# Cross-attention on one core: the K projection in seven 64x64 products in place of eight, from the second head pair on

## What is computed

```python
Q = (x @ W_Q).reshape(1024, 16, 64); K = (ctx @ W_K).reshape(6404, 16, 64); V = (ctx @ W_V).reshape(6404, 16, 64)
attn = softmax(Q K^T / 8, over the 6404 keys)              # per head
out = concat_heads(attn @ V) @ W_O + x
out = (out - mean(out)) / sqrt(var(out) + 1e-5)            # per row
```

## Time and profile before

| | |
|---|---|
| median of 3 runs | 1600.99 us (1600.53 to 1601.82) |
| the profiled execution's own time | 1601.11 us |
| its span in the profile | 1599.3 us |
| granted clock of TensorE, mean | 0.999 |
| TensorE busy | 1590.5 us (99%) |
| VectorE busy | 1314.6 us (82%) |
| ScalarE busy | 835.4 us (52%) |
| GpSimd busy | 64.2 us (4%) |

### The profile page before, as it was taken

The page is one execution under the profiler, slowest core; times in us unless marked ns, Lnnn a source line. Parts: engine busy times, 40 slices in busy tenths (PEclk is TensorE's granted clock), DMA queues, the critical chain, the costliest instruction groups (busy, mean ns, idle before and its releaser), DMA issues.

```text
span 1599.3 us, 39500 instructions
## 1 busy us (share of the span) xinstructions
PE 1590.5 (99%) x17484; PEld 1073.0 (67%) x17484; DVE 1314.6 (82%) x1229; ACT 835.4 (52%) x828; POOL 64.2 (4%) x41
## 2 busy tenths in 40 slices
PE   9999999999999999999999999999999999999998
PEld 4576677766777667766677666776677766777435
DVE  7788788887888788887798878988789887888877
ACT  4445554555545555456544565445654455544653
POOL 0001000010000001000010000000000000000100
PEclk9999999999999999999999999999999999999999
DMA  4000000000000000000000000000000000000000
GB/s 162 3 2 9 1 2 9 2 10 1 10 2 1 10 1 10 2 1 9 1 10 2 2 9 2 10 2 2 9 1 10 2 9 2 1 10 2 9 2 15
DMA packets 13006, 14.26 MB, mean 9 GB/s; under 512 B 4784, under 2 KB 8624, under 8 KB 12832
## 3 DMA queue, kind: packets, MB, share of 16 engines
q1 hardware_dynamic: 12544, 11.36, 2.3%
q10 hardware_dynamic: 288, 0.33, 0.1%
HBM read 10.60 MB, written 0.59 MB: 7 GB/s over the span
## 4 chain that ended last, share of the span: by engine, by line
PE 98%; DVE 1%; ACT 0%; issue 0%; DVEq 0%; ACTq 0%
PE o_ps L484 44%; PE s_ps L467 42%; PE w_ps L549 6%; PE w_ps L532 5%; PE s_ps L616 0%; DVE inv_sum L943 0%; DVE y L976 0%; DVE stats L963 0%; PE w_ps L564 0%; DVE y L959 0%; PE w_ps L607 0%; DVE inv_sum L809 0%; DVE sums L835 0%; DVE limits L985 0%; DVE k_all L809 0%
## 5 line engine op out<-in xcount | busy, mean ns | idle before, releaser
L728 ACT ACTIVATE probs<-s_ps 128x1024 f32<-128x1024 f32 x801 | 822.5, 1027 | 737.1 <-PE s_ps L467 737.1
L835 DVE TENSOR_TENSOR sums<-sums,probs 128x1024 f32<-128x1024 f32 x785 | 968.0, 1233 | 213.7 <-ACT probs L728 205.5
L484 PE MATMUL o_ps<-probs,v_all 64*64 64x512 f32 x6408 | 942.9, 589 | 0.0
L467 PE MATMUL s_ps<-q_sb,k_all 64*64 64x512 f32 x6408 | 942.8, 589 | 0.0
L467 PEld LDWEIGHTS s_ps<-q_sb,k_all 64*64 64x64 f32 x6408 | 447.8, 133 | 238.9 <-issue 39.0
L484 PEld LDWEIGHTS o_ps<-probs,v_all 64*64 64x64 f32 x6408 | 424.8, 133 | 204.9 <-issue 33.6
L532 PEld LDWEIGHTS w_ps<-wv_sb,ctx_all 64*64 64x64 f32 x3176 | 122.4, 132 | 30.6 <-issue 1.7
L809 DVE TENSOR_REDUCE k_all<-w_ps 128x512 f32<-128x1024 f32 (+2 forms) x104 | 122.8, 1181 | 16.0 <-PE w_ps L549 14.9
L809 DVE TENSOR_REDUCE v_all<-w_ps 128x512 f32<-128x1024 f32 (+2 forms) x103 | 121.8, 1182 | 15.8 <-PE w_ps L532 15.7
L532 PE MATMUL w_ps<-wv_sb,ctx_all 64*64 64x128 f32 x3176 | 120.0, 269 | 0.1
L549 PE MATMUL w_ps<-ctx_all,wk_sb 64*64 64x512 f32 (+2 forms) x832 | 119.3, 573 | 0.0
(11 more groups left out here) (85 smaller groups left out, 119.5 us busy)
## 6 DMA issues: line engine op xcount, KB each, us to landing
inv_sum<-inv_dram SPq DMA_DIRECT2D x30, 128.0 KB, 2.9
ctx_all<-in_ctxT SPq DMA_DIRECT2D x11, 256.0 KB, 5.1
quad_rows<-quad_sums SPq DMA_DIRECT2D x60, 4.0 KB, 1.8
x_sb<-in_x SPq DMA_DIRECT2D x1, 512.0 KB, 10.1
wo_sb<-in_wo SPq DMA_DIRECT2D x1, 512.0 KB, 11.3
left_rows<-p_left SPq DMA_DIRECT2D x30, 8.0 KB
inv_left<-inv_dram SPq DMA_DIRECT2D x30, 8.0 KB
wq_sb<-in_wq SPq DMA_DIRECT2D x1, 448.0 KB, 6.4
```

Source lines behind the costliest of these rows:

```text
L467: last = nc.tensor.matmul(s_ps[part(half), u % 2, head * QH:(head + 1) * QH], k_all[part(head), c * P + half * DH:c * P + (half + 1) * DH] ...
L484: last = nc.tensor.matmul(o_ps[part(head), rows, :], v_all[part(rows), c, part(head)], probs[part(rows), u % RING, head * QH:(head + 1) * QH],
L728: nc.scalar.activation(probs[:, u % RING, :], s_ps[:, u % 2, :], ACT.Exp, scale=SCALE).then_inc(probs_ready, 1)
L835: nc.vector.tensor_tensor(out=sums[0:rows, t % 2, :], in0=sums[0:rows, t % 2, :], in1=probs[0:rows, u % RING, :], op=ALU.add).then_inc(sum ...
```

## The change

For every full block of 512 keys of pairs 1 to 7 (12 blocks a pair, 84 in all) the K projection is done by Strassen's scheme: seven products of 64 x 64 by 64 x 128 for each half of the keys, 14 matmuls of 128 columns in place of four of 512. Its parts:

- **First part, kind "r"** (`seven_first`, eight matmuls, two on each array), in the unit where K stood (c % 4 == 0). ScalarE copies its parts that lie on the wrong half of partitions, or are needed in several places, to `crossed` (`cross`, three copies).
- **Second part, kind "k"** (`seven_second`, six matmuls), two units later (c % 4 == 2). V moves from there to one unit later, c % 4 == 3. At the end of a pass with h = 1 the steps are r 38, k 40, v 41, r 42, k 44, v 45.
- **VectorE** (`take_seven`) runs in the unit of the second part: two differences within `crossed` (128 x 128), then a subtraction, a reduction and a subtraction that read `w_ps`; the last one counts up `work_ready`, on which V's matmuls wait.
- **GpSimd and SyncE** form sums of quarters of the context once, in the first pass (`form_keys`, four additions for each of 12 blocks; the quarters on the other half of partitions are loaded by SyncE before each block, the results stored to `forms_dram`), and later load one block of them (128 x 768) for each K block. GpSimd forms differences of the weights once a pair.
- The keys of a block lie in k_all in another order for each head, which `product` undoes in choosing V's chunk (`key_chunk`).

The diff, cut to what matters for the time:

```diff
+    NEXT_STEPS = (0, 36, 38, 40, 41, 42, 44, 45)
...
             at = c - 2 if t == 0 else c
+            if by_seven(pair, at // 4 + 2) and at % 4 in (0, 2):
+                return ("rk"[at % 4 // 2], pair, at // 4 + 2)
             if at >= 0 and at % 4 == 0 and at // 4 + 2 < BLOCKS:
                 return ("k", pair, at // 4 + 2)
-            if at >= 2 and at % 4 == 2 and at // 4 + 2 < BLOCKS:
+            if at >= 2 and at % 4 == (2 if t == 0 else 3) and at // 4 + 2 < BLOCKS:
                 return ("v", pair, at // 4 + 2)
-        elif pair + 1 < PAIRS and c in (0, 36, 38, 40, 42, 44):
-            n = (0, 36, 38, 40, 42, 44).index(c)
-            return (("q", "q", "k", "v", "k", "v")[n], pair + 1, (0, 1, 0, 0, 1, 1)[n])
+        elif pair + 1 < PAIRS and c in NEXT_STEPS:
+            n = NEXT_STEPS.index(c)
+            return ("qqrkvrkv"[n], pair + 1, (0, 1, 0, 0, 0, 1, 1, 1)[n])
...
+            READY[found] = READY[before] + (before[0] != "r") if len(COUNT) > 1 else 1
...
+            load_turned(0)
+            for b in range(FULL_BLOCKS):
+                if b == LEFT_BEHIND:
+                    load_left(0)
+                store_forms(b)
+                if b + 1 < FULL_BLOCKS:
+                    load_turned(b + 1)
...
+            for b in range(FULL_BLOCKS):
+                form_keys(b)
...
+            def seven_first(found):
...
+                pe.wait_ge(work_ready, READY[found] - 1)
+                pe.wait_ge(w_forms_ready, pair)
+                pe.wait_ge(c_forms_loaded[n % 2], 16 * (n // 2 + 1))
+                for i in range(2):
+                    g = part(1 - i)
+                    nc.tensor.matmul(main[g, 0, 1, :], w_form(one, 0, 1 - i), form(one, pair, b, i, 0), start=True, stop=True)
+                    nc.tensor.matmul(extra[g, 0, :], w_form(two, 5, i), form(two, pair, b, i, 2), start=True, stop=True)
+                for i in range(2):
+                    h = part(i)
+                    at = pair * P + i * DH
+                    nc.tensor.matmul(main[h, 1, 1, :], wk_sb[part(one), at:at + DH], form(one, pair, b, i, 1),
+                                     start=True, stop=True)
+                    last = nc.tensor.matmul(m1[h, :], w_form(two, 3, i), form(two, pair, b, i, 0), start=True, stop=True)
+                last.then_inc(work_done, 1)
+            def seven_second(found):
...
+                pe.wait_ge(crossed_ready, 3 * (n + 1))
+                for i in range(2):
+                    nc.tensor.matmul(extra[part(i), 1, :], w_form(two, 4, i), form(two, pair, b, i, 1), start=True, stop=True)
+                for i in range(2):
+                    at = b * BK + 2 * i * P
+                    nc.tensor.matmul(main[part(i), 1, 0, :], w_form(one, 1, i), form(one, pair, b, i, 2), start=True, stop=True)
+                    last = nc.tensor.matmul(main[part(1 - i), 0, 0, :], w_form(one, 2, 1 - i), ctx_all[part(one), at:at + P],
+                                            start=True, stop=True)
+                last.then_inc(work_done, 1)
...
+            def take_seven(found):
...
+                dve.wait_ge(crossed_ready, 3 * (n + 1))
+                nc.vector.tensor_tensor(out=crossed[:, m4, :], in0=crossed[:, m4, :], in1=crossed[:, 0, :],
+                                        op=ALU.subtract).then_inc(crossed_summed, 1)
+                dve.wait_ge(crossed_summed, 2 * n + 1)
+                nc.vector.tensor_tensor(out=crossed[:, 0, :], in0=crossed[:, m3, :], in1=crossed[:, m1, :],
+                                        op=ALU.subtract).then_inc(crossed_summed, 1)
+                dve.wait_ge(crossed_summed, 2 * (n + 1))
+                dve.wait_ge(work_done, COUNT[found])
+                nc.vector.tensor_tensor(out=target[:, :, 0, :], in0=both, in1=main[:, :, 0, :],
+                                        op=ALU.subtract).then_inc(seven_step, 1)
+                nc.vector.tensor_reduce(out=target[:, :, 1, :], in_=main.rearrange("p j s k -> p j k s"), axis=AX.X,
+                                        op=ALU.add)
+                dve.wait_ge(seven_step, n + 1)
+                nc.vector.tensor_tensor(out=target[:, :, 0, :], in0=target[:, :, 0, :], in1=extra,
+                                        op=ALU.subtract).then_inc(work_ready, 1)
```

More of the change, by code:

```diff
@@ new lines, in load_turned_w @@
+            def load_turned_w(pair):
+                if pair > 1:
+                    sp.wait_ge(work_done, COUNT["k", pair - 1, FULL_BLOCKS - 1])
+                for half in range(2):
+                    sp.dma_start(w_forms[part(half), 0, :], w_k[part(1 - half), pair * P:(pair + 1) * P]
+                                 ).then_inc(turned_w_loaded, 16)
+            load_turned(0)
[5 more added lines that the diff above has]
+                    load_turned(b + 1)
@@ L384, in _ @@
                     load_left(t + 1)
+                if h == 0:
+                    for b in range(6, FULL_BLOCKS):
+                        load_forms(pair, b)
             def general():
@@ L483, in product @@
                     for head in range(2):
[L484 removed]
+                        last = nc.tensor.matmul(o_ps[part(head), rows, :],
+                                                v_all[part(rows), key_chunk(t, c, head), part(head)],
                                                 probs[part(rows), u % RING, head * QH:(head + 1) * QH],
```

197 lines of the change are left out of this document (172 added, 25 removed).

## The result

The changed kernel takes **1699.83 us** (median; 1696.05 to 1700.69 in 4 runs) against 1600.76 us (1600.35 to 1601.82 in 4 runs) of the kernel before on the same chip: ratio 1.0613, 95% interval 1.0595 to 1.0632. The profiled execution took 1700.69 us for a span of 1698.9 us, at a mean granted clock of 0.997.

A forecast was written before the change was run, and what follows sets the result against it. TensorE bounds the kernel (busy 1590.5 of 1599.3 us). Block terms 95.8 + 11.6 less 7.9 give +99.5; 1601.1 + 99.5 + 19.6 (extras) + 6 (first pass) = 1726 us, range 1690 to 1765.

The forecast's parts named there:

- TensorE's work, -7.9: TensorE's K projection: fourteen short matmuls cost 0.76 us against 0.86, 0.094 us less for each of 84 blocks.
- The wait in front of V, 1.14 a block: TensorE stands still before V until VectorE's last subtraction ends: 1.14 us in each of 84 blocks, 95.8 us.
- The wait of the first part, 0.15 a block: The next first part on TensorE waits for V's reduction on VectorE: 0.15 us, 77 times, 11.6 us.
- The extras, 19.6: Blocks with extra VectorE work: turn and left keys +9.4, inversion +7.4, GpSimd's scaling colliding with adds +2.8 us.
- GpSimd's lock: GpSimd's scaling lengthens a VectorE add once a pass: 0 to 1.0 us, taken as 0.4, seven times, +2.8.
- The first pass, +6: GpSimd's additions for the forms in pass 0 make VectorE's adds give way: 0 to 18 us, taken as 6.
- SyncE's chain, "covered": SyncE's loads and stores of forms are over by 127 us, before the inversion at 143.26 needs its rows: no cost.
- the signs by which I'd have been wrong: Profile signs against the forecast: V 4.6 us after its scores, TensorE waiting elsewhere, pass 0 over 18 us longer.
- The first (sums in time, 1593 to 1597): Rival: VectorE's sums end before TensorE reaches V, so no wait and a faster kernel, 1593 to 1597 us; chance 0.03.
- The second (arrays that don't go on alone): Rival: TensorE's second part costs its longer half, 0.44 us; with the wait covered 1602 us, no change; chance 0.03.
- The third (a smaller wait, 1620 to 1690): Rival: TensorE's wait before V is only 0.2 to 0.8 us a block, 1620 to 1690 us; chance 0.08.
- The fourth (above 1765): Rival: VectorE or the first pass becomes the bound, time above 1765 us; chance 0.06.

The follow-up runs named there:

- The second: Changed kernel with VectorE's add of the unit before the second part put behind the last subtraction, the second-part unit's add behind V's reduction: 1636.83 us, ratio 1.0215.
- the third: Changed kernel with two more waiting 128 x 128 differences into a spare tile on VectorE, between the second difference and the sums: 1758.96 us, ratio 1.0981.
- the first: Kernel before with its eight products, K moved to the change's second-part unit and V one unit behind it: 1610.21 us, ratio 1.0061.
- the twelfth: Kernel of the eleventh with the left keys' add earlier in passes with h = 1 from the second of them on: 1604.65 us, ratio 1.0023.
- the seventh: Changed kernel with the edits of The second, The fourth run and 6 together: 1623.42 us, ratio 1.0143.
- The fourth run: Changed kernel with SyncE moving the rows of pass 0's sums before it waits for the last block of forms: 1691.44 us, ratio 1.0565.
- 6: Kernel of The fourth run with TensorE's first part and V issued behind the product of their unit: 1645.65 us, ratio 1.0279.
- 8: Kernel of the seventh with the turn of the sums in unit 1 and the fold in unit 5: 1622.23 us, ratio 1.0136.
- the ninth: Kernel of 8 with two of VectorE's adds behind the sums and two behind V's reduction: 1633.24 us, ratio 1.0201.
- the tenth: Kernel of the ninth with each block's two differences on GpSimd in place of VectorE, GpSimd's scaling one unit later: 1629.05 us, ratio 1.0174.
- 5: Changed kernel with the edits of The second and The fourth run, plus the turn in unit 1 and the fold in unit 5: 1625.67 us, ratio 1.0156.
- the eleventh: Kernel of 8 with each block's two differences on GpSimd in place of VectorE: 1607.13 us, ratio 1.0039.

## Why the prediction was right

The step that decides, V waiting for a last subtraction that stands behind B's add on VectorE, was right. The second shows it from one side (the add moved away, 63 us less), the third from the other (0.63 us more on the chain, 0.65 more a block), the first that the new places without the long chain cost only 9. V's loads waited for L1074 84 times, and the differences started 3.47 after B's scores where I said 3.5. The total lay in my range, but 26 us below my value of 1726, and the terms didn't all hold:

- **TensorE's work, -7.9.** Right. Without waits the block measures 8.49 us (the distances of the changed kernel less its wait) or 8.50 (the twelfth) against 8.60: 0.10 and not 0.094. The second part costs 0.25 on average here, in front of a wait, and 0.32 in the seventh and the twelfth; I said 0.33.
- **The wait in front of V, 1.14 a block.** Too long by 0.13 to 0.19. VectorE's operations were as forecast: differences 0.29, last subtraction 0.41, reduction 0.68. Two links weren't. The add starts 2.33 after the scores and not 2.41. And the hand-over from VectorE's last operation to the first matmul is 0.06 us (472.57 to 472.63; 0.05 to 0.06 in all 84 blocks), where I took 0.24 from the one group in the earlier trace rows. That was a misreading. The weight loads of that group start at 71.77, 0.06 behind VectorE's end at 71.71, and its first matmul starts at 71.96 because TensorE was busy until then with a group of scores, which starts 0.86 us earlier:

```profile
71.10 1.04 PE L467 MATMUL s_ps<-q_sb,k_all 64*64 64x512 f32 x8
```

  V starts 5.52 after B's scores, I said 5.77.
- **The wait of the first part, 0.15 a block.** It doesn't show in regular blocks (the first part starts 0.86 after A's scores, as a group without a wait). It rested on the same hand-over, with a margin of 0.15 that 0.18 less removes. Both waits and the shorter second part, less 0.05 that the distance from V to the next product is longer than forecast, are the 0.35 of 9.81 against 9.46. In the sum that is 99.5 against 72, or 27 us: the whole error of the sum and a little more.
- **The extras, 19.6.** 19.3 in all, with another split: left keys 0.94 and turn 0.76 where I had 0.67 each, inversion 1.05 (1.06), GpSimd's lock 0 (0.4). The lock meets A's add and not B's: that add took 1.73 us at 467.19, and B's scores had only just begun.
- **The first pass, +6.** Pass 0 cost 0.5. VectorE's busy time in pass 0 went from 94.5 to 102.8 us of 114, so its adds did give way to GpSimd, but the slack in front of the work that waits for a reduction took it all.
- **SyncE's chain, "covered".** Wrong, and worth 9 us. I let it be free by 127 us by adding 3.2 to 6 us of GpSimd and one load of 2.9 per block. The timeline of GpSimd at its second and third block shows a period of 11:

```profile
35.11 1.86 POOL L570 TENSOR_TENSOR c_forms<-ctx_all,crossed 64x512 f32<-64x512 f32 x1 [5.24 <-DMA c_forms<-in_ctxT]
...
46.16 1.96 POOL L570 TENSOR_TENSOR c_forms<-ctx_all,crossed 64x512 f32<-64x512 f32 x1 [5.05 <-DMA c_forms<-in_ctxT]
```

  The additions were as forecast, but behind each block GpSimd waits some 5 us for the next turned quarters: SyncE issues a store and three loads for them, one after the other, and I had counted one load of 2.9. The chain ran until 148.6. I named the inversion's wait as what would follow, "a few us once"; it was 6.6, and the clock's 2.2 behind it I had not thought of. The fourth run takes both away. A wait of TensorE in front of the scores was among the signs by which I'd have been wrong, and here it stood.

That the 6 us of pass 0 didn't come and these 9 us did partly cancels, which is luck. So is some of the distance to the end of the range: without the delay by SyncE's chain the changed kernel takes 1691.44 (the fourth run), 1.4 us above my lower bound of 1690.

**The rivals.** The first (sums in time, 1593 to 1597) needs an order that the change doesn't have; the seventh builds it and its regular block does show the gain, but no run came under 1604.65. The second (arrays that don't go on alone) is refuted: in the block above, the product's first matmuls start at 469.90 on the arrays that are done, and the second part's last one starts at 470.03; and the second part costs 0.25 to 0.32 and not the 0.44 of its longer half. The rule of the Trainium skill that matmuls start and end in the order of the program, page "TensorE: Matmul & The Clock Gate", section "The mechanism", is not what the starts in this trace show. The third (a smaller wait, 1620 to 1690) has the right direction: the wait is 0.95 to 1.01 in place of 1.14. But it asked for 0.2 to 0.8 and a time under 1690, and the reason was the hand-over and not more overlap. The fourth (above 1765) came to nothing.

In the experiments my ranges lay far too low in runs 2, 6, 7 and 8, by the same step: I looked at the regular block and took the blocks with the fold, the inversion, the scaling and the left keys to be covered. There VectorE has no slack left. In the ninth I missed the wait that the regular block itself would get, and the tenth's range built on the ninth's. Runs 1, 3 and 5 lay 2 us above their ranges; 4, 11 and 12 lay in them. What shows VectorE's lack is the eleventh, which gives VectorE 0.63 us a block and wins 15 us where the regular block wins nothing.

## What to carry to other kernels

Fewer products on the engine that bounds the kernel save 0.1 us a block here; the result that they need costs ten times that if it stands in another engine's list behind an operation that isn't urgent. Before such a change, write down what stands ahead of the first urgent operation and behind the last one on every engine and queue, and look at the blocks that carry something extra, not only at the regular one. An operation that is put off comes back in front of the next block: putting off helps only as far as the engine has time over, and moving work to an idle engine helps beyond that. And before a duration between two engines is read from one place, look what the waiting engine was doing: it may have been busy.

## What the runs showed of the hardware

- **The clock after a wait.** TensorE stood still for 6.63 us, after which the granted clock was 0.50 (1.2 GHz) and three groups cost 1.76, 1.71 and 1.35 us in place of 0.86. The changed kernel's waits of about 1 us in every block, and of 2.0 us seven times, left it at 1.00. In the third run, with 1.6 us in every block, one of 2.6 us was followed by 0.50 in four passes of seven, at 1.7 us each.
- **GpSimd beside VectorE.** A difference of 128 columns takes GpSimd 0.45 us alone and 1.32 beside VectorE's adds. The second difference of a block is mostly beside them in the twelfth run and mostly alone in the tenth (min/median/max in ns):

```profile
L618 POOL TENSOR_TENSOR crossed<-crossed x84: 453/1319/1327, 195.6 to 1469.8; 128x128 f32<-128x128 f32 x84
```

```profile
L615 POOL TENSOR_TENSOR crossed<-crossed x84: 454/458/1323, 195.5 to 1493.8; 128x128 f32<-128x128 f32 x84
```

  VectorE pays little for it: three adds in a row took 3.94 us beside it (430.06 in the twelfth) against 3.87 without. At 458.69 in the twelfth such a difference started during VectorE's third add, which ended at 459.69, and was over at 460.01; so most of its length seems to be a wait for that add, which no run tested. The slower engine was still the better place.
- **The hand-over** from VectorE to a waiting matmul was 0.05 to 0.06 us, at V in all 84 blocks of the changed kernel and at the first part in the 14 in which it waits.
